# The 39 table gathers of a group, issued in three bursts of 13 rather than in four of 9 to 10

## The reference

```python
e = stack([tbl_f[ids[:, f]] for f in range(39)], axis=1)        # 2048 x 39 x 16
x0 = xk = e
for W, b in ((w0, b0), (w1, b1), (w2, b2)):                     # W: 39 x fields of xk x 128
    z = relu(einsum('bhd,bkd,hks->bsd', x0, xk, W) + b)         # 128 outputs
    # layers 0, 1: xk = first 64 outputs, the other 64 go to the logits; layer 2: all 128
logit = sum over d of the kept parts                            # 2048 x 256
h = relu([logit, dense_ctx] @ W_top1 + b_top1)
y = relu(h @ W_top2 + b_top2) @ W_top3                          # 2048 x 1
```

## Time and profile before

| | before |
|---|---|
| median of 3 runs | 2581.95 us (2576.76 to 2585.32) |
| the profiled execution, own time | 2581.92 us |
| its span | 2580.1 us |
| PE busy | 2440.5 us (95%) |
| DVE busy | 2271.5 us (88%) |
| POOL busy | 1557.8 us (60%) |
| ACT busy | 1175.9 us (46%) |
| gathers (L345) | 624, 700.6 us busy, mean 1123 ns |
| PE idle before the transposes (L667) | 87.6 us in 16 waits |

### The profile page before, as it was taken

The page is one execution under the profiler, slowest core; times in us unless marked ns, Lnnn a source line. Parts: engine busy times, 40 slices in busy tenths (PEclk is TensorE's granted clock), DMA queues, the critical chain, the costliest instruction groups (busy, mean ns, idle before and its releaser), DMA issues.

```text
span 2580.1 us, 25984 instructions
## 1 busy us (share of the span) xinstructions
PE 2440.5 (95%) x7712; PEld 1427.7 (55%) x7712; DVE 2271.5 (88%) x1356; ACT 1175.9 (46%) x1414; POOL 1557.8 (60%) x1030
## 2 busy tenths in 40 slices
PE   0399999999999999999999999999999999999999
PEld 0255555555555555555555555555555555555553
DVE  0489999998999999999999999999999999999960
ACT  0144444444444444454444454444444454444442
POOL 6466676576667657666766676666667666743340
PEclk9899999999999999999999999999999999999999
DMA  2978888887888888788888888888898888878810
GB/s 59 233 168 199 205 192 188 211 200 178 198 206 192 187 211 199 184 192 209 199 183 211 205 194 180 208 208 180 196 215 200 177 206 209 191 181 211 202 30 0
DMA packets 262600, 477.02 MB, mean 185 GB/s; under 512 B 19372, under 2 KB 37676, under 8 KB 262502
## 3 DMA queue, kind: packets, MB, share of 16 engines
q1 hardware_dynamic: 141622, 271.05, 44.6%
q10 hardware_dynamic: 100480, 200.29, 32.9%
q0 software_dynamic: 20480, 5.47, 1.3%
HBM read 468.99 MB, written 7.74 MB: 185 GB/s over the span
## 4 chain that ended last, share of the span: by engine, by line
PE 67%; POOL 10%; issue 8%; DVE 6%; DMA 5%; ACT 2%; another core or an unknown queue 1%; SPq 0%; POOLq 0%; DVEq 0%; ACTq 0%
PE z L686 34%; PE z L709 30%; POOL emb L345 5%; DVE prod L412 4%; DMA emb<-in_tbl,idx 4%; POOL pair_lo L210 4%; PE xk L768 1%; PE z L768 1%; ACT pair_hi L526 1%; POOL half_parts L206 1%; DVE logit L442 1%; DVE pair_lo L210 1%; PE turned L667 1%; DMA x_diag<-x_transposed 1%
## 5 line engine op out<-in xcount | busy, mean ns | idle before, releaser
L412 DVE TENSOR_TENSOR prod<-x_pairs,xk 128x2048 f32<-128x2048 f32 x640 | 1438.6, 2284 | 98.7 <-PE z L709 70.1
L686 PE MATMUL z<-prod,w_plain 128*128 128x512 f32 (+2 forms) x2944 | 1388.1, 595 | 43.2 <-issue 25.9
L526 ACT CAST pair_hi<-prod 128x1024 fp32r<-128x1024 f32 x703 | 735.5, 1046 | 1099.6 <-PE z L709 772.5
L210 POOL TENSOR_TENSOR pair_lo<-prod,pair_hi 128x1024 fp32r<-128x1024 f32 x320 | 763.8, 2387 | 650.9 <-ACT pair_hi L526 634.5
L686 PEld LDWEIGHTS z<-prod,w_plain 128*128 128x128 f32 (+2 forms) x2944 | 557.5, 190 | 479.0 <-issue 402.7
L345 POOL DMA_INDIRECT emb<-in_tbl,idx x624 | 700.6, 1123 | 189.5 <-issue 174.6
L709 PE MATMUL z<-pair_hi,w_lo 128*128 128x512 f32 (+1 forms) x1408 | 787.5, 559 | 2.4 <-DVE pair_lo L210 1.8
L709 PE MATMUL z<-pair_hi,w_hi 128*128 128x512 f32 (+1 forms) x1408 | 556.0, 395 | 0.0
L709 PE MATMUL z<-pair_lo,w_hi 128*128 128x512 f32 (+1 forms) x1408 | 555.4, 394 | 0.0
L210 DVE TENSOR_TENSOR pair_lo<-prod,pair_hi 128x1024 fp32r<-128x1024 f32 (+1 forms) x384 | 467.9, 1219 | 48.7 <-ACT pair_hi L526 44.1
L709 PEld LDWEIGHTS z<-pair_hi,w_lo 128*128 128x128 f32 (+1 forms) x1408 | 265.7, 189 | 298.1 <-POOL pair_lo L210 138.7
(11 more groups left out here) (50 smaller groups left out, 566.3 us busy)
## 6 DMA issues: line engine op xcount, KB each, us to landing
x_pairs<-x_transposed ACTq DMA_DIRECT2D x64, 2432.0 KB
x_pairs<-x_transposed SPq DMA_DIRECT2D x64, 2432.0 KB
x_diag<-x_transposed SPq DMA_DIRECT2D x128, 546.0 KB
x_diag<-x_transposed ACTq DMA_DIRECT2D x64, 546.0 KB
x_pairs<-x_transposed SPq DMA_DIRECT2D x64, 256.0 KB
emb<-in_tbl,idx POOLq DMA_INDIRECT x624
x_diag<-x_transposed SPq DMA_DIRECT2D x128, 78.0 KB
x_transposed<-stage SPq DMA_DIRECT2D x32, 156.0 KB
```

Of the source, the lines that this page charges most:

```text
L210: engine.tensor_tensor(pair_lo[0:rows, pair % PAIR_RING], held[0:rows, at:at + 2, :], pair_hi[0:rows, pair % PAIR_RING].bitcast(F32), ALU. ...
L412: nc.vector.tensor_tensor(prod[0:rows, pos % RING, 0:n, :], a, xk.unsqueeze(1).broadcast_to([rows, n, N]), ALU.mult).then_inc(prod_ready, 1)
L526: nc.scalar.copy(pair_hi[0:rows, pair % PAIR_RING], held[:, at:at + 2, :]).then_inc(hi_ready, 1)
L686: ins = nc.tensor.matmul(z[n][:], w, held[0:rows, i, :], start=(k == 0 and i == plain[0]), stop=(k == last_slot and not here and i == plai ...
```

## The change

Two constants; the code around them is the same, and it takes all its counts from them.

```diff
-GATHERS_AHEAD = 30
-GATHERS_AT = [range(30, F), range(0, 10), range(10, 20), range(20, 30)]
+GATHERS_AHEAD = F
+GATHERS_AT = [[], range(0, 13), range(13, 26), range(26, F)]
```

## The result

The changed kernel takes 2604.77 us (median of 4 runs, 2601.24 to 2611.16) against 2582.2 us before. The ratio is 1.0097, with a 95% interval of 1.0078 to 1.0115: slower by 1%, or 22.6 us. Forecast was 2551 us and faster, with a range that ended at 2645.

The account below looks back on a forecast made before the run. The prediction took PE, busy 95% of the span, as the bound. From 2581.92 us it took 27.3 us of waits and 7.5 us of low clock and added 4 us for late bursts: 2551 us, range 2543 to 2645 us.

Parts of the forecast that it names:

- What bounds the kernel: PE, busy 95% of the span; at layer 2's first pair it has nothing to spare, POOL 1.1 us behind bursts of ten.
- What the change removes: PE's 15 later waits for gathers before the transposes, 27.3 us, and the low clock, 7.5 us: 34.8 us in all.
- the low clock: PE's fall to 1.2 GHz behind some waits for gathers before the transposes; claimed to vanish with them, 7.5 us.
- No other wait of about 2 us: Claim that PE has no other such wait in the loop, the reason for taking the 7.5 us in full.
- The length of the burst: POOL's bursts of 13: last three gathers take 1.78, 0.95 and 1.25 us, ending 4.9 us behind the old end.
- When does the 13th gather land?: POOL's wait behind a burst: last packet at 548.1 us, POOL let on at 549.0, 3.2 us behind the issue.
- s: How late POOL starts its low parts behind a burst; each of 42 bursts costs s - 0.2 us, likeliest 0.1 us.
- Break-even: Lateness of POOL behind each burst from which the change loses: 1.0 us, a landing 4.3 us behind the last issue.
- The slower one: Rival: the burst on POOL's queue lands behind SP's bands of `x0_diag`, s = 2.0, 2623 us; chance 0.31.
- The gather that doesn't queue: Rival: the 13th gather lands at the lower bound, 547.4 us, POOL's slack stays, 2547 us; chance 0.15.

## Why the prediction was wrong

**What bounds the kernel: right.** PE, with no slack at layer 2's first pair, and 1.1 us of slack on POOL behind a burst of ten. This was the place, and it decided.

**What the change removes: right.** 27.1 us of waits went (27.3 forecast), and the kernel that only removes them lost 34.6 us in its 14 stretches (32.8 of the forecast 34.8 fall in them; the rest is the first wait, ahead of them). That the low clock would go with them held there, where no stretch is longer than 147.5 us, but not in the changed kernel: three stretches with new waits of 2 us still had it, 152.5 to 152.8 us in place of 150.7 or so, some 6 us together. "No other wait of about 2 us" was true only as long as no burst was late.

**The length of the burst: right.** 19.0 us, with the three gathers at 1.78, 0.94 and 1.24 us. The reading that a gather is held by DVE's low part holds over the whole trace before: the 228 gathers that start in a low part take 1.42 us on average, up to 1.79, and those that start in a DVE product 0.95 us.

**"When does the 13th gather land?": this step failed**, in its last term. In the packets of the changed kernel the last ones of q0 move 2.5 us behind the last issue on average over the 42 bursts (1.6 to 3.7), with the end of q10's at 2.4. The prediction had 2.3 us, at the end of ACT's transfer and just ahead of SP's: right. It then added 0.9 us from the last packet to POOL's release, read from a burst of ten. In the changed kernel it is 2.0 us on average: for the burst shown, the packets end at 552.5 us and the release is at 554.4. So the release came 4.6 us behind the issue and not 3.2. The low part started 4.75 us behind it, where ACT alone would have let it start at 3.29, as in the kernel with the wait moved: s was 1.5 us, where the prediction had 0.3 at most. PE's wait was 1.4 us and the stretch grew by 1.1 us per burst (what gives the 0.3 us back was not looked into), in place of 0.1, so that 42 bursts cost some 45 us in place of 4. With the 6 us of low clock, 3 to 4 us for stretches that without late bursts are 147.6 us long and not the forecast 147.35, and 3 us outside the 14 stretches, that is the gap from 2551 to 2604.

**Where I chose badly.** The slack was 1.1 us, and the landing had bounds of 1.6 and 6.95 us. The value in between, 3.2 us, hung on a lag read once, in another state of the queues. Break-even was at 0.2 + 34.8/42 = 1.0 us of lateness, which is 4.2 us behind the issue (the prediction has 4.3), and the releases lie at 4.6 on average, just past it. A forecast of 0.57 for faster was more than such a margin bears.

**The rivals.** The slower one gave 2623 us and was nearest, but its mechanism, a burst behind SP's bands, is refuted for 13 gathers and only seen in the packets for 15. That its sign and size came near is luck. The gather that doesn't queue is refuted: behind chunk 1, with ACT's transfer drained, the release comes 1.3 to 2.5 us behind the issue, and with it running 4.3 to 5.6. By the Trainium skill's rule (DMA: Bandwidth & Descriptors, section "Queues, rings and completion order") that an engine takes turns between its queue rows, I would have expected no such difference; the trace does not bear that out here.

**What stays open**: what fills the 2 us from last packet to release. It is 0.3 to 0.4 us on average when ACT's transfer has drained before the last issue. Where the last packets move with the end of that transfer, it is 1.2, 1.6 and 2.0 us for bursts of 11, 12 and 13. The same section of the Trainium skill says that a semaphore's increment lands only after every earlier write from its DMA engine, across its queues. That would fit the longer times beside ACT's transfer. But 1.0 us behind a burst of ten, with the transfer still going on, and the growth from 11 to 13, with all of them ending together with it, speak against it as the whole story. No run settles it.

## What to carry to other kernels

A wait for a DMA stands in front of everything that its engine does next, whoever needs the data. Ask which instruction really needs it, and put the wait there: here a move of 8 us down the queue turned +1.0% into -1.1% with the same DMAs. And look at what bulk loads a small transfer runs beside before you count on a slack of about 1 us: here its landing moved with the end of such a load, not with its own issue, and a duration read at one place of the schedule did not hold 5 us later.

## What the runs showed of the hardware that I had not expected

- The last of a burst of small gathers lands at nearly the same moment, whether it was issued 16.2 or 19.0 us into the burst (low part at 23.1 and 23.8 us), and 6 us later when it is issued behind the next bulk load (29.8 us at 21.6 us).
- From a gather's last packet to its release: 0.3 to 0.4 us with ACT's transfer drained, 1.0 us in a burst of ten, 1.2 to 2.0 us where both end together.
- PE's clock fell to the 1.2 GHz level behind 4 of the 15 waits at the transposes before the change, each of 1.95 to 1.96 us, and not behind others of 2.1 and 2.3 us; a stretch with such a fall was 1.6 to 2.2 us longer than the usual one.
